# Expert stages of a macaron block: exponentials of the key scores multiplied into the grid, heads summed by accumulating transfers, and new orders on four engines

## What is computed

```python
q = einsum('btd,ed->bte', h, W_q)                       # two halves x and y, 4 heads of 64
sim = einsum('pbthn,hkpn->pbthk', q, keys)              # 64 key scores per head and half
scores_xy, idx_xy = top_k(sim, 8)
all_scores = (sx[..., :, None] + sy[..., None, :]).reshape(b, t, 4, 64)
all_idx = (ix[..., :, None] * 64 + iy[..., None, :]).reshape(b, t, 4, 64)
scores, pk = top_k(all_scores, 8)
indices = take_along_axis(all_idx, pk)                  # clamped to 1024 experts by the gather
w = silu(einsum('btd,bthkd->bthk', h, down_embed[indices]) * softmax(scores))
experts = einsum('bthk,bthkd->btd', w, up_embed[indices])
dense = einsum('bti,di->btd', silu(einsum('btd,id->bti', h, W_up)), W_down)
return dense + experts
```

## Time and profile before

| | us |
|---|---|
| median of 3 runs (4009.54 to 4012.56) | 4010.79 |
| the profiled execution | 4008.62 |
| its span, first to last instruction | 4006.8 |

### The profile page before, as it was taken

The page is one execution under the profiler, slowest core; times in us unless marked ns, Lnnn a source line. Parts: engine busy times, 40 slices in busy tenths (PEclk is TensorE's granted clock), DMA queues, the critical chain, the costliest instruction groups (busy, mean ns, idle before and its releaser), DMA issues. The chain is left out here.

```text
span 4006.8 us, 81018 instructions
## 1 busy us (share of the span) xinstructions
PE 3796.5 (95%) x28440; PEld 3314.4 (83%) x28440; DVE 3198.6 (80%) x7738; ACT 3098.6 (77%) x7882; POOL 2701.5 (67%) x2202
## 2 busy tenths in 40 slices
PE   7999999999979999999998799999999997999989
PEld 6888888888858888888886688888888887898878
DVE  7888888888758888888875788888888877756667
ACT  6888888888759999999996688888888877632166
POOL 7888888888655554655541788888888866512266
PEclk9999999999989999999999899999999998999999
DMA  2000000000010000000000100000000003331342
GB/s 66 17 17 17 17 17 17 17 17 17 9 44 18 13 23 14 22 23 13 23 7 18 64 17 17 17 17 17 17 17 17 17 12 98 122 105 53 127 151 90
DMA packets 135061, 141.90 MB, mean 35 GB/s; under 512 B 8672, under 2 KB 131968, under 8 KB 134656
## 3 DMA queue, kind: packets, MB, share of 16 engines
q1 hardware_dynamic: 134656, 136.71, 10.7%
HBM read 80.06 MB, written 56.62 MB: 34 GB/s over the span
## 5 line engine op out<-in xcount | busy, mean ns | idle before, releaser
L300 POOL TENSOR_TENSOR f_grid<-f_sim 128x1024 f32<-128x1024 f32 x512 | 969.4, 1910 | 0.1
L1512 ACT ACTIVATE a_ex<-a_p_s,a_mneg 128x128 f32<-128x128 f32 x2048 | 728.2, 409 | 89.9 <-DVE a_mneg L1566 89.9
L686 DVE SCALAR_TENSOR_TENSOR f_p_u<-f_grid,f_te,f_p_dot 128x1024 f32<-128x1024 f32 x512 | 653.2, 1276 | 111.7 <-PE f_p_dot L106 65.3
L308 POOL TENSOR_TENSOR f_q<-f_q 128x1024 f32<-128x1024 f32 x256 | 607.9, 2386 | 123.1 <-ACT f_q L558 121.0
L695 DVE SCALAR_TENSOR_TENSOR f_q<-f_p_u,f_rz,f_grid 128x1024 f32<-128x1024 f32 x512 | 650.9, 1271 | 0.4
L539 ACT ACTIVATE f_grid<-f_grid,f_negm 128x1024 f32<-128x1024 f32 x512 | 559.2, 1142 | 0.0
L1512 ACT ACTIVATION_READ_ACCUMULATOR a_ex<-a_p_s,a_mneg 128x1 f32 x2048 | 508.8, 248 | 0.0
L443 PE MATMUL f_p_y<-f_eup,f_wT 128*128 128x256 f32 x2048 | 472.9, 379 | 0.0
L438 PE MATMUL f_p_y<-f_wdn,f_hs 128*128 128x256 f32 x2048 | 468.4, 382 | 0.0
L443 PEld LDWEIGHTS f_p_y<-f_eup,f_wT 128*128 128x128 f32 x2048 | 388.5, 190 | 57.7
L438 PEld LDWEIGHTS f_p_y<-f_wdn,f_hs 128*128 128x128 f32 x2048 | 378.8, 190 | 49.7
(11 more groups left out here) (646 smaller groups left out, 11029.3 us busy)
## 6 DMA issues: line engine op xcount, KB each, us to landing
x_f<-f_yt SPq DMA_DIRECT2D x64, 256.0 KB, 2.1
f_xt<-x SPq DMA_DIRECT2D x32, 256.0 KB, 2.9
a_xt<-x_f SPq DMA_DIRECT2D x16, 512.0 KB, 3.8
x_a<-a_yt SPq DMA_DIRECT2D x16, 512.0 KB, 2.9
f_xt<-x_a SPq DMA_DIRECT2D x32, 256.0 KB, 2.9
c_xt<-x_f SPq DMA_DIRECT2D x16, 512.0 KB, 4.7
x_c<-c_yt SPq DMA_DIRECT2D x16, 512.0 KB, 3.1
b1p_xt<-x_c SPq DMA_DIRECT2D x16, 512.0 KB, 3.9
```

The source lines that it names most:

```text
L300: g_grid.mark(pool.tensor_tensor(grid[v][:, hd, :].rearrange("p (i j) -> p i j", i=XROWS), sx[:, hd, :].unsqueeze(2).to_broadcast([P, XROW ...
L308: g_pair.mark(pool.tensor_tensor(q[v][:, 2 * k, :], q[v][:, 2 * k, :], q[v][:, 2 * k + 1, :], ALU.add), f"{v}{k}")
L686: d_mask.mark(dve.scalar_tensor_tensor(out=p_u[:], in0=grid[v][:, hd, :], scalar=te[:, v, hd, TOP - 1:TOP], in1=p_dot[:], op0=ALU.is_ge, o ...
L1512: last = act.activation(ex[t.step % 2][:, i, n, :], p_s[i][:, n, :], ACT.Exp, bias=mneg[:, i, n:n + 1], accum_out=z[t.step % 2][:, i, n:n ...
```

## The change

Four things are changed in `expert_ffn`; the other stages are untouched.

- ScalarE no longer exponentiates the grid, the list and no longer copies the scores. It exponentiates the key scores, 64 at a time with the negative maximum of those 64 as bias, from p_sim to `ex` (16 activations per step). The maxima come from a new reduce on VectorE (`lowest`), straight from p_sim. Grid and candidates are then products of exponentials: GpSimd's `scores` and `pairs` multiply where they added, and `best` yields the exponentiated list at once.
- The four heads are summed by transfers: GpSimd issues three per tile, each adding q of one head (128 x 1024 numbers, 512 KB) onto head 0, and each waits for the one before to have landed.
- TensorE transposes one sum and not two: 4 matmuls per group where there were 8.
- The `step(t)` of all four engines is written in another order. `weights` is split into `front`, `third` and `back`.

The transfers' semaphores `s_add` are made once around all stages. The diff, cut to its core (in GpSimd's `pairs` and `scores`, ALU.add has become ALU.mult and sim ex; `listed`, `next_exps` and the old `exps` are gone):

Buffers:

```diff
-        sim = m.sbuf("sim", V, 2 * HEADS * KEYS)
+        ex = m.sbuf("ex", V, 2 * HEADS * KEYS)
...
-        tops, te = (m.sbuf(k, V, HEADS, 2 * TOP) for k in ("tops", "te"))
+        te = m.sbuf("te", V, HEADS, 2 * TOP)
...
-        negm, z, rz = (m.sbuf(k, V, HEADS) for k in ("negm", "z", "rz"))
+        negm = m.sbuf("negm", V, 2 * HEADS)
+        z, rz = (m.sbuf(k, V, HEADS) for k in ("z", "rz"))
```

GpSimd:

```diff
 def summed(t, v, k):
-    a_silu.wait(pool, t, f"back{v}" if k else f"front{v}")
-    g_pair.mark(pool.tensor_tensor(q[v][:, 2 * k, :], q[v][:, 2 * k, :], q[v][:, 2 * k + 1, :], ALU.add),
-                f"{v}{k}")
+    a_silu.wait(pool, t, (f"front{v}", f"clamped{v}", f"back{v}")[k])
+    if k:
+        s_add[v][k - 1].wait(pool, t)
+    s_add[v][k].mark(pool.dma_start(q[v][:, 0, :], q[v][:, k + 1, :], accum_op=ALU.add))
...
 def step(t):
     after = (t + 1).exists(last=count)
+    if (t - 1).exists():
+        summed(t - 1, 1, 2)
     tails(t, 0)
     if after:
+        scores(t + 1, 0, (0, 1))
+    summed(t, 0, 0)
+    if after:
         pairs(t + 1, 0)
-        scores(t + 1, 0, (0, 1))
+        scores(t + 1, 0, (2,))
     clamps(t, 0)
-    summed(t, 0, 0)
+    if after:
+        scores(t + 1, 0, (3,))
     summed(t, 0, 1)
     tails(t, 1)
     if after:
-        scores(t + 1, 0, (2,))
+        scores(t + 1, 1, (0,))
+    summed(t, 0, 2)
+    if after:
+        scores(t + 1, 1, (1,))
+    summed(t, 1, 0)
+    if after:
         pairs(t + 1, 1)
-        scores(t + 1, 0, (3,))
+        scores(t + 1, 1, (2,))
     clamps(t, 1)
     if after:
-        scores(t + 1, 1, (0,))
-    summed(t, 1, 0)
+        scores(t + 1, 1, (3,))
     summed(t, 1, 1)
     if (t + 3).exists(last=count):
         root(t + 3)
-    if after:
-        scores(t + 1, 1, (1, 2, 3))
```

TensorE:

```diff
 def turn_w(t, v, k):
     if k == 0:
-        g_pair.wait(pe, t, f"{v}1")
+        s_add[v][HEADS - 2].wait(pe, t)
...
     for e in range(HALF):
-        for hd in (0, 2):
-            last = pe.matmul(p_wT[:, e, :], q[v][:, hd, (k * HALF + e) * P:(k * HALF + e + 1) * P],
-                             ident[:], is_transpose=True, start=hd == 0, stop=hd == 2)
+        last = pe.transpose(p_wT[:, e, :], q[v][:, 0, (k * HALF + e) * P:(k * HALF + e + 1) * P], ident[:])
...
 def step(t):
-    if before:
-        turn_w(t - 1, 1, 0)
+    hidden(t, 0)
     if after:
         similar(t + 1, 1)
-    hidden(t, 0)
+    if before:
+        dense(t - 1, 1)
+        turn_w(t - 1, 1, 0)
+    hidden(t, 1)
     if before:
         turn_w(t - 1, 1, 1)
-        dense(t - 1, 1)
         experts(t - 1, 1, 0)
+    if later:
+        turn_h(t + 2)
     dots(t, 1)
     if before:
         experts(t - 1, 1, 1)
-    hidden(t, 1)
+    hidden(t, 2)
+    hidden(t, 3)
+    dense(t, 0)
+    turn_w(t, 0, 0)
     if later:
-        turn_h(t + 2)
-    hidden(t, 2)
-    turn_w(t, 0, 0)
-    hidden(t, 3)
+        similar(t + 2, 0)
     turn_w(t, 0, 1)
-    dense(t, 0)
     if after:
         dots(t + 1, 0)
     experts(t, 0, 0)
     experts(t, 0, 1)
-    if later:
-        similar(t + 2, 0)
```

ScalarE:

```diff
-def similar(t, v):
+def exps(t, v):
     t_sim.wait(act, t, str(v))
+    d_neg.wait(act, t, str(v))
     if (t - 1).exists():
         g_grid.wait(act, t - 1, f"{v}3")
         d_top.wait(act, t - 1, f"maxes{v}")
-    a_sim.mark(act.copy(sim[:, v, :], p_sim[:]), str(v))
+    for n in range(2 * HEADS):
+        last = act.activation(ex[:, v, n * KEYS:(n + 1) * KEYS], p_sim[:, n * KEYS:(n + 1) * KEYS],
+                              ACT.Exp, bias=negm[:, v, n:n + 1])
+    a_ex.mark(last, str(v))
...
 def step(t):
-    exps(t, 1, (0, 1))
+    if later:
+        normed(t + 2)
+    if after:
+        exps(t + 1, 1)
+    hidden(t, 0)
+    if before:
+        turned(t - 1, 1, 0)
+    front(t, 0)
+    hidden(t, 1)
     if before:
         turned(t - 1, 1, 1)
-    exps(t, 1, (2, 3))
-    if after:
-        similar(t + 1, 1)
-    hidden(t, 0)
-    if later:
-        normed(t + 2)
-    weights(t, 0)
-    hidden(t, 1)
+    third(t, 0)
+    back(t, 0)
     if later:
         turn_h(t + 2)
     hidden(t, 2)
+    hidden(t, 3)
+    front(t, 1)
+    third(t, 1)
     turned(t, 0, 0)
-    hidden(t, 3)
+    back(t, 1)
     turned(t, 0, 1)
-    weights(t, 1)
-    if after:
-        next_exps(t + 1)
+    if later:
+        exps(t + 2, 0)
```

VectorE:

```diff
+def lowest(t, v):
+    t_sim.wait(dve, t, str(v))
+    d_neg.mark(dve.tensor_reduce(negm[:, v, :], p_sim[:].rearrange("p (n k) -> p n k", k=KEYS), AX.X,
+                                 ALU.max, negate=True), str(v))
...
 def step(t):
     for v in range(V):
         mask(t, v, 0)
+        weigh(t, v, 0)
         if before:
             output(t - 1, v)
-        weigh(t, v, 0)
+        if v == 0 and after:
+            lowest(t + 1, 1)
+        if v == 1 and later:
+            turned(t + 2)
...
         if after:
             best(t + 1, v)
-        if v == 0:
-            inverse(t, 1)
-    if later:
-        turned(t + 2)
+            inverse(t + 1, v)
     if (t + 3).exists(last=count):
         front(t + 3)
-    if after:
-        inverse(t + 1, 0)
+    if later:
+        lowest(t + 2, 0)
```

More of the change, by code:

```diff
@@ L335, in _ @@
                 pairs(first, 0)
-                scores(first, 0, (0, 1))
+                scores(first, 0, range(HEADS))
                 pairs(first, 1)
-                scores(first, 0, (2, 3))
                 root(first + 2)
@@ L362, in step @@
                         root(t + 3)
-                    if after:
-                        scores(t + 1, 1, (1, 2, 3))
                 turns(pool, count, unroll, step)
+                summed(end, 1, 2)
             @block.tensor
@@ L383, in similar @@
                     else:
-                        a_sim.wait(pe, t, "0")
+                        a_ex.wait(pe, t, "0")
                     for c in range(DC):
@@ L490, in step @@
                     experts(t, 0, 1)
-                    if later:
-                        similar(t + 2, 0)
                 turns(pe, count, unroll, step)
-                for k in range(2):
-                    turn_w(end, 1, k)
                 dense(end, 1)
+                turn_w(end, 1, 0)
+                turn_w(end, 1, 1)
                 for k in range(2):
@@ L729, in _ @@
                 lower(1)
+                lowest(first, 0)
                 front(first + 1)
                 maxes(first, 0, range(3 * HEADS))
-                best(first, 0)
                 lower(2)
                 lower(3)
+                lowest(first, 1)
+                best(first, 0)
+                inverse(first, 0)
                 maxes(first, 1, range(3 * HEADS))
-                best(first, 1)
                 front(first + 2)
                 turned(first + 1)
-                inverse(first, 0)
+                lowest(first + 1, 0)
+                best(first, 1)
+                inverse(first, 1)
                 def step(t):
```

93 lines of the change are left out of this document (36 added, 57 removed).

## The result

The changed kernel takes 4204.49 us (median of 4 runs, 4200.71 to 4206.89) against 4010.34 us for the kernel before: the ratio is 1.0482, with a 95% interval of 1.0464 to 1.05. It is slower, by 194 us. The forecast was 4192 us, with a range of 4060 to 4400.

A forecast was written before the change was run, and what follows sets the result against it. TensorE was taken to bound the 33.3 us step; a new loop of waits, 35.8 plus 0.4 for transfers, gave 36.2. (36.2 - 33.3) x 61 = 177, plus about 5, gave 4192 us, range 4060 to 4400.

The forecast's parts named there:

- What bounds the kernel before: Expert stages: TensorE is the bound, idle 0.9 us of a 33.3 us step; other engines have 4 to 5.5 us spare.
- The loop: Between VectorE's second reduces, through GpSimd's clamp, ScalarE's copy and TensorE: 11.70 + 9.59 + 3.31 + 1.14 + 9.94 = 35.7 us.
- GpSimd's part: Wait chain from tile 1's maxima through pairs, grid product and clamp: 3.31 us per step.
- The second branch: Reduce, exponentials, table load, silu, hidden(1), transposes and experts until tile 1's dots: 8.5 us against 8.52 for VectorE's rest.
- The transfers: GpSimd's queue waits for landings; free up to 4.4 us each, taken as 4.9, adding 0.4 us: period 36.2.
- The sum: Expert stages: (36.2 - 33.3) x 61 = 177 us plus about 5, giving 4190 profiled and 4192 as median.
- About 5 for the ends: Ends of the expert stages, where the last transfers stand alone: about 5 us added in all.
- Slow transfers: Rival: landing takes 7.6 us or issue 2 us, GpSimd's queue is the loop; period 39.0, 4360 us; chance 0.20.
- Faster, if the clamp does not bind: Rival: VectorE becomes the bound with one stall of some 2.2 us; period 32.3, 3947 us; chance 0.13.
- only a part of the chain: Rival: the chain's pieces overlap more than forecast; period 33.7 to 35, 4030 to 4110 us; chance 0.10.
- no difference: Rival: new waits take back TensorE's saved 1.7 us per step; time within 8 us; chance 0.04.
- What would show it: Signs in the changed profile: period near 36 us, named waits on TensorE, VectorE and GpSimd, ScalarE's share some 55%.

The follow-up runs named there:

- experiments 1 and 2: 1: changed kernel with ScalarE's copy of the weights ahead of the third silu, 4113.22 us; 2: changed kernel with GpSimd's clamp ahead of the grid product, 4117.98 us.
- Experiment 3: Changed kernel with VectorE's second reduce, lowest(t+1, 1), moved behind the second mask and its two maxima; 4210.39 us.
- experiments 5 and 6: Both on the copy-first kernel (4113.22 us): 5, TensorE's similar ahead of hidden, 4119.63 us; 6, GpSimd's transfer 2 of tile 0 ahead of a grid product, 4080.73 us.

## Why the prediction was right, point by point

- *What bounds the kernel before, and that no saving by count would show.* Right: TensorE's busy time fell by 50 us in 500 (per step by only 1.1 us, the rest is that steps are longer), and the step got longer.
- *The loop.* Shown by experiments 1 and 2, which cut it at two links and gained 1.6 us a step each, and by 3, where removing a wait that is not a link of its own gave nothing. The parts measured 11.61 (forecast 11.70), 9.56 (9.59), 3.65 (3.31), 1.18 with the latency to TensorE (1.24, if the 0.10 that the prediction has in its last part is counted here) and 9.76 (9.84), in all 35.76. GpSimd's part was too short by 0.3 us, since the clamp took 0.64 us and not 0.26; a transfer had been issued ahead of it (last section). The other four were each too long by 0.03 to 0.09.
- *The second branch.* Right and as close as said: in the trace the dots of tile 1 start at 623.13, 8.53 us after the reduce, with TensorE busy ahead of them, and VectorE's tail dots end at 623.03. The eight exponentials took 1.74 us, not 1.9 to 2.0, and the terms that the prediction lists add up to 8.3 to 8.4, not to its 8.5; the gaps between them, which it left out, made up for both. Experiment 3 rests on this.
- *The transfers.* D, the time from issue to landing, was taken as 4.9 us; the page of the profile has 4.8, and from issue to the next issue 5.40 passed in the step and 5.1 where they stand alone. Issue takes 0.60 to 0.69 us of GpSimd's queue where I had 1.0. By these rows the candidates could have started 9.4 us after tile 1's first mask (0.97 + 5.40 + 2.45 + 0.60), and the maxima are done after 9.56; they start 0.09 us behind the maxima, of which the prediction has 0.08 in GpSimd's part. So the term was to be 0.4 us and is nothing. By the Trainium skill's figures (DMA: Bandwidth & Descriptors, Anatomy of one DMA, SWDGE path), an estimate of 3.2 us for such a transfer, the term would have been nothing; the measured 4.8 us decides against 3.2, though the term it leads to, nothing, is the one that came.
- *The sum.* 4192 was 12 us under the median because two errors of opposite sign nearly cancelled, and that is luck. The forecast for the two profiled executions was 61 x 2.9 + 5 = 182 us, and they lie 191 apart. The 58 steady steps gave 144.7 us where the forecast has 58 x 2.9 = 168.2, since the period is 35.75 and 35.80 and not 36.2: 23.5 less. The starts and ends hold the other three steps of the 61; they took 37.7 us more than before, where the forecast has 3 x 2.9 + 5 = 13.7: 24 more than forecast. "About 5 for the ends" was the term that failed. Longer steps, 9.3 us, were put at nothing. In step 0 TensorE now waits 10.39 us at once for hidden's silu, where its longest wait behind the loading of the weights was 7.03 us before, and at the end of a stage it waits 3.26 us for the last transfer, which follows the one before it by 5.09 us. How the 37.7 us divide among such waits was not worked out.
- *The rivals.* Slow transfers: excluded, D was 4.8, although they set the step once the clamp no longer did (experiments 5 and 6). Faster, if the clamp does not bind: with the clamp moved away the kernel still took 4113 and 4118, so the 3947 of that rival was too low; behind the first loop stood a second one of 34.17 us, through the transfers, that I had not walked. The other two, only a part of the chain (33.7 to 35) and no difference, are excluded by the period of 35.76.
- *What would show it.* TensorE's wait on the copy was 1.4 us (its weight load 1.8), a little under the 1.5 to 3 forecast; VectorE's 2.4 (2 to 3.5); ScalarE's share 57% (55%); GpSimd's wait before the third transfer 1.7 (1 to 3). TensorE's clock was to stay at full speed. It did in the steady steps of the first stage (1.00), but not in four of the second, whose mean is 0.99.

## What to carry to other kernels

Follow the queues around one full step before adding up busy time: when several engines get less work and the order changes, the loop of waits is the period, and one small instruction in the wrong place (a clamp of 0.25 to 0.64 us ahead of a copy that frees a PSUM buffer) can cost 90 us. A wait that stands out in the table is not by that on the loop (2.4 us per step gave nothing, moving one call elsewhere 1.6), a second loop often stands close behind the first, and the same move gains in one order and costs in another, so re-time each. Look at the start and end of a stage by themselves when a chain of dependent transfers is put in, and at rare longer steps, which the median of a step does not show.
